# A graph attention layer and a mixture of experts on one core: loads, step order, the end of the attention half and the router's first pick rearranged

## The reference

```python
# half 1, for each batch; x is (16, 512, 128), adj is (16, 512, 512) of int32
h = layernorm(x)
Wh = h @ W.T                       # 128 x 128
e = leaky_relu((Wh @ a1)[:, None] + (Wh @ a2)[None, :], 0.2)
att = softmax(where(adj > 0, e, -9e15))
x = x + elu(att @ Wh)
# half 2
x2 = layernorm(x)
logits = mean over nodes(x2) @ Wr + br           # (16, 8)
w = softmax(softmax(logits) * scale)             # scale: capacity over the load summed over all batches
top_w, top_i = top_k(w, 2); top_w = softmax(top_w)
y = sum over the 2 experts: top_w * (gelu(x2 @ W1[e] + b1[e]) @ W2[e] + b2[e])   # 128 -> 256 -> 128
x = x + layernorm(y + x2) * gamma + beta
```

## Time and profile before

| | us |
|---|---|
| median of 3 runs (334.18 to 336.31) | 335.86 |
| the profiled execution | 334.51 |
| its span in the trace | 332.7 |
| mean granted clock of TensorE | 0.951 of full speed |

### The profile page before, as it was taken

One profiled execution on the slowest core, in us unless ns is written; L12 is line 12 of the kernel. 1 busy time (PEld: TensorE's weight loads), 2 busy tenths in 40 slices (PEclk: granted clock), 3 DMA queues, 4 the chain that ended last, 5 costly groups with the idle time before them and its releaser, 6 DMA issues. The chain is left out here.

```text
span 332.7 us, 7851 instructions
## 1 busy us (share of the span) xinstructions
PE 269.2 (81%) x1901; PEld 237.0 (71%) x1901; DVE 251.8 (76%) x708; ACT 235.6 (71%) x534; POOL 156.5 (47%) x369
## 2 busy tenths in 40 slices
PE   8619878888778777877896587697999999999960
PEld 3419767787668767876795474376999998998960
DVE  3376888999889888988897876525568868868765
ACT  1234887788878887888888963373878978878731
POOL 2455366776567557765754812002133432342453
PEclk9978999999999999999999987687999999999995
DMA  6972545356444643465113001236245445545222
GB/s 185 343 207 85 187 162 176 117 182 212 172 121 164 217 161 117 167 218 187 38 35 127 32 33 63 99 123 224 97 159 177 157 155 176 173 144 189 96 64 63
DMA packets 51486, 48.27 MB, mean 145 GB/s; under 512 B 2912, under 2 KB 37120, under 8 KB 51456
## 3 DMA queue, kind: packets, MB, share of 16 engines
q1 hardware_dynamic: 51456, 47.94, 43.6%
HBM read 31.67 MB, written 4.20 MB: 108 GB/s over the span
## 5 line engine op out<-in xcount | busy, mean ns | idle before, releaser
L1311 PE MATMUL banks<-whx,prob_t 128*128 128x129 f32 x512 | 64.2, 279 | 0.0
L629 DVE SCALAR_TENSOR_TENSOR logit<-masked_dst,shift_pos,leaky 128x512 f32<-128x512 f32 x64 | 48.0, 750 | 18.8 <-ACT leaky L1047 13.7
L1311 PEld LDWEIGHTS banks<-whx,prob_t 128*128 128x128 f32 x512 | 61.2, 195 | 0.2
L1047 ACT ACTIVATE leaky<-masked_dst,shift_neg 128x512 f32<-128x512 f32 x64 | 47.1, 740 | 13.3 <-POOL shift_neg L506 13.1
L617 DVE CUSTOM_DVE_ANT_0 masked_dst<-mask,banks 128x512 f32<-128x512 bf16 x64 | 42.3, 681 | 2.5 <-PE banks L1274 1.0
L1297 PE MATMUL banks<-ident,logit 128*128 128x128 f32 x256 | 39.8, 279 | 5.4 <-DVE logit L629 3.3
L1274 PE MATMUL banks<-ident,whx 128*128 128x128 f32 x128 | 19.4, 297 | 28.4 <-ACT whx L1038 28.4
L549 POOL TENSOR_SCALAR veps<-mv 128x4 f32<-128x4 f32 x15 | 5.9, 392 | 75.9 <-DVE mv L913 75.9
L1084 ACT ACTIVATE prob_t<-banks 128x512 f32<-128x512 f32 x64 | 35.2, 599 | 7.5 <-PE banks L1297 7.5
L1274 PEld LDWEIGHTS banks<-ident,whx 128*128 128x128 f32 x128 | 16.3, 198 | 31.5 <-ACT whx L1038 31.5
L1181 ACT ACTIVATE logit<-logit,nb,rstd 128x128 f32<-128x128 f32 x60 | 24.7, 483 | 18.9 <-POOL nb L554 18.9
(11 more groups left out here) (151 smaller groups left out, 586.0 us busy)
## 6 DMA issues: line engine op xcount, KB each, us to landing
adj_sb<-in_adj_dram SPq DMA_DIRECT2D x16, 1024.0 KB, 5.3
w_pair<-w_parts SPq DMA_DIRECT2D x30, 256.0 KB, 2.3
x_rows<-in_x_dram SPq DMA_DIRECT2D x16, 256.0 KB, 2.9
x_all<-in_x_dram SPq DMA_DIRECT2D x16, 256.0 KB, 3.2
x_all<-x2s SPq DMA_DIRECT2D x16, 256.0 KB, 2.3
w2r<-in_L_ffn_W_dram SPq DMA_DIRECT2D x32, 128.0 KB, 2.1
out_dram<-prob_t SPq DMA_DIRECT2D x15, 256.0 KB, 2.2
w_raw<-in_L_ffn_W_dram SPq DMA_DIRECT2D x1, 1024.0 KB, 5.5
```

Source lines behind the costliest of these rows:

```text
L629: nc.vector.scalar_tensor_tensor(out=logit[:, t, :], in0=masked_dst[:, t, :], scalar=shift_pos[:, t:t + 1], in1=leaky[:, t, :], op0=ALU.ad ...
L1047: nc.scalar.activation(leaky[:, t, :], masked_dst[:, t, :], ACT.Identity, bias=shift_neg[:, t:t + 1], scale=ALPHA).then_inc(s_leaky, 1)
L1311: last = nc.tensor.matmul(into[:, 0:D + 1], prob_t[:, t, c * P:(c + 1) * P], whx[par][:, c, 2:WHX], start=(c == 0), stop=(c == T - 1))
```

## The change

The diff touches every engine's program. What it does, part by part:
- **Loads.** The GNN weights first, then rows of batches 0 and 1, adj 0, rows 2, adj 1, rows 3, W1 (straight into the low half of w1_parts), x of 0 and 1. The six small loads come behind step 1. In `step`, `keep_x2` stands one place earlier and for the batch three before.
- **First batches** written out on each engine: TensorE transposes batch 0 before it prepares the weights, which now go through dst_ps; one warm-up product instead of four; GpSimd does row_shifts(0) ahead of norms(2); the W1 splits lie in steps 0 and 1.
- **Steady order** new on SyncE, VectorE, ScalarE and TensorE. V is 1.
- **End of the attention half** written out, by tile for batch 15 down to `norm2_last_tile` and `scale_x2_last`; batch 14 shared by VectorE and ScalarE. `stay_warm` is a bfloat16 product, done 0, 4, 4 and 8 times.
- **Router.** The first pick on ScalarE; b1's selection between the first hidden products; the two splits of x2t between router steps.
- **Feed-forward.** Loads of W1 and W2 of batch 2 ahead of the b2 round trip, which has a buffer of its own. TensorE ends with out(14), hidden(15), out(15). VectorE's tail is reordered, with a buffer of its own for z of batch 15.

```diff
-        V = T // 2
+        V = 1
+        WARM = (0, 4, 4, 8)
@@ SyncE
-            load_rows(0, 0)
             (gnn_w_sb, a_src, a_dst)
-            load_adj(0, 0)
-            load_rows(0, 1)
-            load_x(0, 0)
-            load_adj(0, 1)
-            load_x(0, 1)
+            load_rows(0, 0)
+            load_rows(0, 1)
+            load_adj(0, 0)
+            load_rows(0, 2)
+            load_adj(0, 1)
+            load_rows(0, 3)
+            sp.dma_start(w1_parts[:, :, 1, :].bitcast(F32), w1.rearrange("e p f -> p e f")).then_inc(s_w1raw, 16)
+            load_x(0, 0)
+            load_x(0, 1)
...
+            step(0, -1)
+            step(0, 0)
+            step(0, 1)
+            load_small()
+            pipeline(sp, step, 2, LAST, LEAD + FIRST - 2, LAG)
...
             load_w2(1)
+            load_w1(2)
+            load_w2(2)
             sp.wait_ge(s_b2_row, 1)
@@ GpSimd
+            norms(0, 0)
+            norms(0, 1)
+            row_shifts(0, 0)
+            norms(0, 2)
+            pipeline(pool, step, 1, LAST, LEAD + FIRST - 1, LAG)
+            norm2_before_last()
+            for t in range(T):
+                norm2_last_tile(t)
```

```diff
@@ VectorE, start, end of the attention half, router
+            stats1(0, 0)
+            stats1(0, 1)
+            make_mask(0, 0)
+            stats1(0, 2)
+            masked_max(0, 0, 0)
+            masked_max(0, 0, 1)
+            step(0, 0)
+            split_w1_lo(0)
+            step(0, 1)
+            split_w1_lo(1)
+            pipeline(dve, step, 2, B - 2, LEAD + FIRST - 2, (B - 1) - (LAST + 1 - LAG))
...
+            residual_pos_tile(2)
+            residual_neg_tile(2)
+            scale_x2_before_last()
+            stats_tile(2)
+            aggregate_tile(2)
+            residual_pos_tile(3)
+            residual_neg_tile(3)
+            stats_tile(3)
+            aggregate_tile(3)
+            for t in range(T):
+                scale_x2_last(t)
...
             router_steps["shifted"] = rc[0]
+            split_x2t_lo(0, 0)
...
-            e = dve.value_load(top_idx[0:1, 0:1], min_val=0, max_val=E - 1)
-            nc.vector.tensor_copy(w1_pair[0][:, 0], w1_parts[:, e]).then_inc(s_pick[0], 1)
@@ ScalarE, start, end, router
+            copy_xnt(0, 0)
+            act.wait_ge(s_prep_ps, 1)
+            nc.scalar.copy(wh_weights[:], dst_ps[:, 0:D + 2]).then_inc(s_prep, 1)
+            copy_wh(0, 0)
+            copy_xnt(0, 1)
+            copy_wh(0, 1)
...
+            last_normalize(0)
+            probs(0, B - 1, 3)
+            last_normalize(1)
+            copy_x2t(0, B - 4)
+            last_normalize(2)
+            copy_x2t(0, B - 3)
+            last_normalize(3)
+            scale_x2_before_last()
+            copy_x2t(0, B - 2)
...
+            act.wait_ge(s_idx, 1)
+            e = act.value_load(top_idx[0:1, 0:1], min_val=0, max_val=E - 1)
+            act.wait_ge(s_w1lo, 2)
+            nc.scalar.copy(w1_pair[0][:, 0], w1_parts[:, e]).then_inc(s_pick[0], 1)
             act.wait_ge(s_rdve, router_steps["rescaled"])
@@ TensorE, start, turn, end
+            warm_up(1)
+            pe.wait_ge(s_const, 1)
+            transpose_x(0, 0)
+            (weights prepared in dst_ps)
+            project(0, 0)
+            transpose_x(0, 1)
+            spread_dst(0, 0)
...
-                nc.tensor.matmul(lt_ps[0], ones[:], x2t_all[:, 0, :], start=True, stop=True)
+                for _ in range(times):
+                    nc.tensor.matmul(lt_ps[0], mask[:, 0, 0:P], mask[:, 1, :], start=True, stop=True)
...
-            hidden_part(0, 0, (spread_gates, None, mix_b2, None))
+            hidden_part(0, 0, (select_b1, spread_gates, mix_b2, None))
...
-            pipeline(pe, step2, 0, B - 1, 4, 2)
+            pipeline(pe, step2, 0, B - 3, 4, 0)
+            out_part(0, B - 2)
+            hidden_part(0, B - 1)
+            out_part(0, B - 1)
```

436 lines of the change are left out of this document (259 added, 177 removed).

## The result

| | before | changed |
|---|---|---|
| median, us | 335.92 (334.18 to 336.31) | 316.84 (313.17 to 319.19) |
| ratio, 95% interval | | 0.9385 (0.9328 to 0.9443) |
| profiled execution / its span | 334.51 / 332.7 | 319.19 / 317.4 |

The change gains 6.2%, 19.1 us by the medians. The forecast was 306.5 with a range of 299 to 319: the side is right, the time lies inside the range, and more than 10 us of the gain foreseen are missing. The profiled execution, 319.19 us, is the slowest of the four and counts as a slow one (the others took 313.17 to 317.82), so its stages are set beside those of a second profile of the same kernel (a1_after, 318.20 us, span 316.4).

A forecast was written before the change was run, and what follows sets the result against it. VectorE was taken to bound the attention half, TensorE's chain the feed-forward half. Six gains summed to 29.3 us, taking the profiled 334.5 to 305.2; with 1.35 for the median, 306.5 us, range 299 to 319.

The forecast's parts named there:

- the six terms: Gains forecast: start 7.0, steady steps 9.0, end of attention half 4.7, router 1.9, feed-forward half 4.1, tail 2.6 us.
- The tail: After TensorE's end: less VectorE work left, 8.3 us for 10.9; 2.6 won, between 1 and 4.
- The end of the attention half: Last batch tile by tile, two splits gone: 15.5 us against 20.24; 4.7 won, between 3 and 6.
- The main course: Whole kernel: all terms as forecast, 306.5 us, own range 300 to 313; chance 0.60.
- the third: Rival: new order wins nothing in the steady step (10.84 us), the rest stands; 315.5 us, chance 0.12.
- Steady step: 13 attention steps of 10.15 us instead of 10.84, a walked period of 9.85 plus 0.3 small waits; 9.0 us won.
- 0.3 us are lost: Steady step: VectorE waits 0.3 us for the next batch's scores, which need whx and TensorE's turn after the first transposes.
- The second rival: GpSimd's chain sets the steady step, up to 10.55 us; 5.2 us more, 312; chance 0.15.
- The start: Up to batch 2's first logit tile: 37.6 us against 44.57, 7.0 won; batch 0's first tile at 16.4.
- The router: First vector step to first hidden product: 5.75 us against 7.65; 1.9 won, between 0.5 and 2.4.
- The feed-forward half: First hidden product to TensorE's end: 104.3 us against 108.4, W1 of batch 2's landing hidden; 4.1 won.
- no wait there for a W1 load later: Sign in the new profile: after the first hidden product, no wait for a W1 load.

The follow-up runs named there:

- e9: Changed kernel with W1's load put behind the loads of step 1 and its four split pieces moved to steps 2 to 4; 315.33 us, ratio to before 0.9391.
- e4: Changed kernel with V back at 2, so VectorE and ScalarE scale two x2s tiles each; 320.17 us, ratio to before 0.9492.
- e3: Changed kernel with VectorE's mask put back right behind the negative residual, ahead of the statistics; 316.20 us, ratio to before 0.9369.
- e8: Changed kernel with VectorE's x2s tile ahead of the mask and the statistics of batch n+3 behind the first logit tile; 317.49 us, ratio to before 0.9478.
- e5: Changed kernel with the x loads of batches 0 and 1 issued ahead of W1's load; 316.91 us, ratio to before 0.9445.
- e10: Changed kernel with x2s tile ahead of mask, score spreading ahead of logit transposes, x2t copy ahead of first probability tile; 316.24 us, ratio to before 0.9421.
- e1: Changed kernel with b2's store ahead of W1(2) and W2(2), and W1(3) and W2(3) between b2's two broadcasts; 313.17 us, ratio to before 0.9272.
- b1: Kernel before with b2's store ahead of W1(2) and W2(2), and W1(3) and W2(3) between b2's broadcasts; 332.67 us, ratio to before 0.9875.
- e6_warm: Changed kernel with TensorE's warm-up products at (8, 8, 8, 8) instead of (0, 4, 4, 8); 316.84 us, ratio to before 0.9454.
- c_all: Changed kernel with four edits: SyncE's b2 order, x2s tile ahead of mask, longer warm runs, W1's load and splits later; 310.51 us, ratio to before 0.9248.

## Why the prediction was right, and where it was not

**Mechanisms.** Five of the six terms have the right sign. The tail (8.59 for 8.3) came out as walked. The end of the attention half (15.63 for 15.5) came out in part by luck: at the full clock the same program takes 13.95 us there (e9), so the walk was 1.5 too long, and the fall of the clock, which the prediction didn't have here, took 1.7 back. That the total lies in the range of 299 to 319 is luck in part too. The main course had a range of its own, 300 to 313, and 316.84 is outside it; the rival that names this time (the third, 315.5) did not happen, for its steps of 10.84 us came out at 10.28.

**Steady step.** 10.28 for 10.15, 7.3 us for 9.0. That V is worth 0.26 a step, because VectorE's work is on the path, is shown by e4 (0.27); that the mask's old place costs a wait of 0.8 is shown by e3, but not that its removal wins 0.8: its net price is 0.26. "0.3 us are lost" for the spread scores was the term that was small: 0.46 to 0.71, because the transposes of the first logit tile stand ahead. The second rival ("GpSimd's chain sets the step", 312) did not come true in the changed kernel, where GpSimd still waits 0.48 us for the fourth maximum; e8 shows how near it is.

**The start.** 3.5 for 7.0. The landing of the first megabyte was put at 9.5 and came at 11.66, and one collision was missed, row_max behind the mask of batch 1 (1.0 us). Together they make logit(0) 19.39 for 16.4. The wait of step 1 for the rows of batch 4 was foreseen in place and roughly in size (1.8 us up to 24.5; measured 2.44 up to 28.13). They were asked for at 21.16 and took 7.0 us, for 19.3 and 5.2. The step that failed is the use of single landings from the start of before: e5 and e9 show that here bytes count, one megabyte less in front bringing these rows 3.3 to 3.5 us sooner, and an earlier place in the queue nothing.

**The router.** 6.20 for 5.75. At the full clock it takes 5.22 (e3, e9, e10), so the walk was 0.5 too long and the clock's 1.0 was left out. The part that was walked in detail, from the index to the first hidden product, came out: the index is ready at 194.81, the product starts at 196.48, 1.7 us for 1.8, with ScalarE's pick at 195.71 and 0.62 long.

**The feed-forward half.** This is where the forecast failed: "The 4.32 us landing of W1 of batch 2, on the chain before, is hidden, because its load no longer stands behind the b2 round trip." That is true. Two steps behind it fail. Nothing was said of the load that stands there now, W1 of batch 3, which landed at 217.3. And the claim that VectorE, when b2 comes later, "lags but has 1.8 us to spare in every step" left out that the split for batch 3 stands behind the add of b2: it ended at 217.98 and released the product. Counted from start to start, the stall takes 4.2 us (7.71 from the output product to the hidden one for 3.49), the lower clock behind it 2.8 (5.25 for 2.84 and 3.87 for 3.49), and the end of TensorE's work, from the start of hidden(15), 1.0 more than the forecast's (a gap of 1.62 for 1.0 is part of it). These are all of the 8.0 us between 104.3 and 112.33; in a1_after it is 4.1, 1.3 and 1.0. e1 and b1 show that the order around the round trip is the cause: without the stall 106.2. The prediction had named what would show it, "no wait there for a W1 load later", and the profile shows the wait.

## What to carry to other kernels

When a load is taken out from behind a slow round trip, price the next load in the same queue, and on every other engine the work that stands behind the result of the round trip: here the two chains end within 0.6 us of each other. What helped was to ask for the round trip earlier and to cover its own wait, by putting two loads between the store and its reading back. A wait that the profile puts down to one releaser can have two; look at what else the instruction waits for in the program, and when that ended. When a wait is removed in a ring of engines, ask which wait behind it had been covered by it; the gain is the difference. And in a start where the transfer engines are full, count the bytes in front of a load; another order alone did not bring it sooner.

## What was not expected of the hardware

The same idle stretch of TensorE, 2.19 us, was followed by a granted clock of 0.50 (1.2 GHz) in seven profiles (the changed kernel, a1_after, e1 to e5) and of 1.00 in three (e8, e9, e10), with the same instructions behind it; in e3 the clock was back at 1.00 in the router. With the stretch cut to 0.46 or 0.47 it stayed at 1.00 in both profiles that had it (e6_warm, c_all). In these profiles, then, the idle time alone doesn't decide, and without it no fall was seen; what decides was not found. The fall costs up to 2.65 us, 1.0 of it in the router, and is part of the spread of the medians.
